# Second attention of a two-layer gated block on one core: score products moved from padded full-height operands to strips of 32 array rows

## The reference

```python
def _L1_xattn_ref(q, k, v, gamma):            # q = layernorm(x); k = v = ctx
    B, Dq, Lq = q.shape                       # 32, 64, 256
    h = 8; dq = Dq // h                       # 8 heads of 8 rows
    qh = q.reshape(B, h, dq, Lq); kh = k.reshape(B, h, dq, Lk); vh = v.reshape(B, h, dv, Lk)
    qk = jnp.einsum('bhdq,bhdl->bhql', qh, kh) * scale
    sm = jax.nn.softmax(qk, axis=-1)
    ret = jnp.einsum('bhql,bhdl->bhdq', sm, vh)
    return gamma * ret.reshape(B, Dv, Lq)
x = x + jnp.tanh(g_xattn[1]) * _L1_xattn_ref(_layernorm(x, axis=-1), ctx, ctx, gamma)
```

## Time and profile before

| | |
|---|---|
| median of 3 runs | 817.76 us (816.28 to 818.45) |
| span of the profiled execution, first to last instruction | 814.5 us |
| PE busy with matmuls, share of the span | 755.2 us, 93% |
| PE busy with weight loads | 576.9 us, 71% |
| DVE busy | 513.3 us, 63% |
| ACT busy | 435.3 us, 53% |
| POOL busy | 295.0 us, 36% |
| mean granted clock of TensorE | 0.975 of full speed |

### The profile page before, as it was taken

One profiled execution on the slowest core, in us unless ns is written; L12 is line 12 of the kernel. 1 busy time (PEld: TensorE's weight loads), 2 busy tenths in 40 slices (PEclk: granted clock), 3 DMA queues, 4 the chain that ended last, 5 costly groups with the idle time before them and its releaser, 6 DMA issues. The chain is left out here.

```text
span 814.5 us, 16953 instructions
## 1 busy us (share of the span) xinstructions
PE 755.2 (93%) x5377; PEld 576.9 (71%) x5377; DVE 513.3 (63%) x871; ACT 435.3 (53%) x862; POOL 295.0 (36%) x354
## 2 busy tenths in 40 slices
PE   4788889999995999999999999689999999999997
PEld 3677667888985666666666666367787778878776
DVE  3888857897797877887788787462344244253222
ACT  3888834344442777778777787633322332233221
POOL 3455542224446524433533443153222223213222
PEclk9999979999996899999999999889999999999999
DMA  5444410000004433433333331000000000000000
GB/s 146 119 112 128 116 59 1 1 0 0 1 21 127 131 99 97 113 109 94 110 106 100 94 112 44 1 1 1 1 1 27 1 1 26 0 0 0 27 1 27
DMA packets 48093, 43.88 MB, mean 54 GB/s; under 512 B 7860, under 2 KB 46356, under 8 KB 48052
## 3 DMA queue, kind: packets, MB, share of 16 engines
q1 hardware_dynamic: 45892, 37.46, 16.2%
q0 software_dynamic: 2160, 5.90, 2.6%
HBM read 27.99 MB, written 15.07 MB: 53 GB/s over the span
## 5 line engine op out<-in xcount | busy, mean ns | idle before, releaser
L1321 DVE TENSOR_REDUCE a_smax<-a_s 128x4 f32<-128x1024 f32 x128 | 154.4, 1209 | 46.6 <-PE a_s L1255 46.4
L1155 ACT ACTIVATE a_prob<-a_st 128x512 f32<-128x512 f32 x256 | 144.6, 591 | 34.9 <-PE a_st L1243 33.8
L1593 POOL TENSOR_TENSOR f_hs_lo<-f_hid,f_hs_hi 128x512 fp32r<-128x512 f32 (+1 forms) x56 | 73.3, 1308 | 197.4 <-ACT f_hs_hi L1539 197.4
L1243 PE MATMUL a_st<-qop,kop 128*128 128x256 f32 x512 | 120.7, 318 | 1.0 <-DMA qop<-a_neg_t 0.6
L1243 PEld LDWEIGHTS a_st<-qop,kop 128*128 128x128 f32 x512 | 77.2, 189 | 60.3 <-ACT a_prob L1155 44.2
L117 PE MATMUL f_bank<-wd_hi,f_hs_hi 128*128 128x256 f32 (+1 forms) x352 | 104.4, 297 | 7.2 <-POOL f_hs_lo L800 6.2
L1653 DVE TENSOR_TENSOR f_prod<-f_sg,f_bank 128x512 f32<-128x512 f32 x44 | 30.2, 687 | 128.1 <-PE f_bank L119 110.4
L1539 ACT ACTIVATE f_hs_hi<-f_hid 128x512 fp32r<-128x512 f32 (+1 forms) x56 | 35.4, 632 | 139.4 <-PE f_bank L119 99.8
L1255 PE MATMUL a_s<-kop,qop 127*128 127x256 f32 x512 | 104.9, 291 | 4.9 <-DVE a_smax L1321 2.6
L119 PE MATMUL f_bank<-wd_hi,f_hs_lo 128*128 128x256 f32 (+1 forms) x352 | 99.3, 282 | 0.0
L118 PE MATMUL f_bank<-wd_lo,f_hs_hi 128*128 128x256 f32 (+1 forms) x352 | 99.0, 281 | 0.0
(11 more groups left out here) (180 smaller groups left out, 1393.0 us busy)
## 6 DMA issues: line engine op xcount, KB each, us to landing
kop<-kop_rows SPq DMA_DIRECT2D x128, 48.0 KB
qop<-qop_rows SPq DMA_DIRECT2D x128, 48.0 KB
kop_rows<-k_hi SPq DMA_DIRECT2D x32, 128.0 KB, 2.3
qop_rows<-q_hi POOLq DMA_DIRECT2D x30, 128.0 KB, 2.6
x_all<-in_x SPq DMA_DIRECT2D x4, 512.0 KB, 4.7
ctx_t<-in_ctx SPq DMA_DIRECT2D x16, 128.0 KB, 2.0
kop_rows<-k_lo SPq DMA_DIRECT2D x16, 128.0 KB, 2.3
a_ctx<-in_ctx SPq DMA_DIRECT2D x16, 128.0 KB, 2.1
```

The source lines that it names most:

```text
L1155: act.activation(prob[:, u % 8], st_ps[u % 2][:], ACT.Exp, scale=SCALE1).then_inc(prob_ready, 1)
L1243: mm = pe.matmul(st_ps[u % 2][:, c * D:(c + 1) * D], lhsT=kop[t.slot][:, u // 4, c * P:(c + 1) * P], rhs=qop[t.slot][:, u // 4, u % 4], st ...
L1321: dve.tensor_reduce(smax[:, v.slot, 2 * j:2 * j + 2].rearrange("p u q -> p (u q)"), s_ps[j % 2][:].rearrange("p u (q n) -> p (u q) n", q=2 ...
L1593: pool.tensor_tensor(hs[1][0:r, c % 2], hid[0:r, c % 2], raw(hs[0][0:r, c % 2]), ALU.subtract).then_inc(hs_ready, 1)
```

## The change

The query operand loses its padding: `qop` is `[P, QUADS, D]`, with each unit's rows in the unit's own strip, as in `kop`. Its memset falls away. Both score products read only one strip: 24 rows for `s`, and 25 for `st`, as the row of maxima now lies in row 24 of each strip (partitions 24, 56, 88, 120). `tile_position` puts each product on the 32 array rows of its strip. The `s` products of a step are done in another order (`opposite`: unit u^2 in the place of u), and the four matmuls of a place alternate: st, s, st, s. The store of the maximum and the order within `neg` follow suit. All waits of a place now stand ahead of its four matmuls, and `st_done` is raised by the third of them.

```diff
-MROW = P - 1
+KROWS = QROWS + 1
...
-        self.q.append(sb(f"qop{n}", [P, QUADS, 4, D], F32R))
+        self.q.append(sb(f"qop{n}", [P, QUADS, D], F32R))
...
-        pool.memset(raw(self.k[slot][:]), 1.0)
-        pool.memset(raw(self.q[slot][:]), 0.0).then_inc(self.cleared, 1)
+        pool.memset(raw(self.k[slot][:]), 1.0).then_inc(self.cleared, 1)
...
-            dst = self.q[t.slot][v * UROWS:v * UROWS + QROWS, quads, v]
+            dst = self.q[t.slot][v * UROWS:v * UROWS + QROWS, quads]
...
+        def opposite(u):
+
+            return u ^ 2
...
-                sp.dma_start(raw(qop[t.slot][MROW:P, 2 * h:2 * h + 2]), neg_t[:, h]).then_inc(max_loaded[h][t.slot], 16)
+                sp.dma_start(raw(qop[t.slot][QROWS:P:UROWS, 2 * h:2 * h + 2]), neg_t[:, h]).then_inc(max_loaded[h][t.slot], 16)
...
-                        for c in range(DC):
-                            mm = pe.matmul(st_ps[u % 2][:, c * D:(c + 1) * D], lhsT=kop[t.slot][:, u // 4, c * P:(c + 1) * P],
-                                           rhs=qop[t.slot][:, u // 4, u % 4], start=True, stop=True)
-                        mm.then_inc(st_done, 1)
...
-                        for q in range(2):
-                            mm = pe.matmul(s_ps[j % 2][:, k, q * D:(q + 1) * D], lhsT=qop[v.slot][0:MROW, u // 4, u % 4, q * P:(q + 1) * P],
-                                           rhs=kop[v.slot][0:MROW, u // 4], start=True, stop=True)
-                        if k == 1:
-                            mm.then_inc(s_done, 1)
+                    for c in range(DC):
+                        if t.inside(TILES):
+                            strip = slice(u % 4 * UROWS, u % 4 * UROWS + KROWS)
+                            st = pe.matmul(st_ps[u % 2][:, c * D:(c + 1) * D], lhsT=kop[t.slot][strip, u // 4, c * P:(c + 1) * P],
+                                           rhs=qop[t.slot][strip, u // 4], start=True, stop=True, tile_position=(u % 4 * UROWS, 0))
+                        if v.inside(TILES):
+                            w = opposite(u)
+                            strip = slice(w % 4 * UROWS, w % 4 * UROWS + QROWS)
+                            sm = pe.matmul(s_ps[j % 2][:, k, c * D:(c + 1) * D], lhsT=qop[v.slot][strip, w // 4, c * P:(c + 1) * P],
+                                           rhs=kop[v.slot][strip, w // 4], start=True, stop=True, tile_position=(w % 4 * UROWS, 0))
+                    if t.inside(TILES):
+                        st.then_inc(st_done, 1)
+                    if v.inside(TILES) and k == 1:
+                        sm.then_inc(s_done, 1)
...
-                    src = smax[:, w_.slot, 8 * h:8 * h + 8].rearrange("p u q -> p q u")
+                    src = smax[:, w_.slot, 8 * h:8 * h + 8].rearrange("p (g v) q -> p q v g", g=2)
...
-                    dve.tensor_scalar(neg[:, h], src, -1.0, None, ALU.mult).then_inc(neg_ready, 1)
+                    dve.tensor_scalar(neg[:, h].rearrange("p q (v g) -> p q v g", g=2), src, -1.0, None, ALU.mult).then_inc(neg_ready, 1)
...
-                        dve.tensor_reduce(smax[:, v.slot, 2 * j:2 * j + 2].rearrange("p u q -> p (u q)"),
+                        dve.tensor_reduce(smax[:, v.slot, opposite(2 * j):opposite(2 * j) + 2].rearrange("p u q -> p (u q)"),
```

## The result

The changed kernel took 827.71, 827.83, 894.87 and 896.86 us, a median of 861.35 against 817.76 before. Over the two shorter executions alone the ratio is 1.0123 (interval 1.0103 to 1.0143), 1.2% slower; by the median of all four it is 5.3% slower. The two long ones have a mean granted clock of 0.79, the two short ones of 0.89, so the time goes with how long the clock stayed at half, and the spread is part of the result. The profiled execution is the first, with a span of 826.0 us. I had forecast 781.

The account below looks back on a forecast made before the run. PE was taken to set the pace at 15.84 us a step; minus 3.84 for sharing, plus 0.87 for borders and 0.4 for waits gives 13.3, saving 37 us over 14.8 steps: 781 us, range 767 to 819.

Parts of the forecast that it names:

- the step of 13.3 us: Changed stage at full clock: PE's 12.9 us plus 0.4 for waits, against 15.84 before, saving 37 us.
- Pairs stream together: Neighbouring score matmuls in different row strips share the array: 0.24 us saved per unit, 3.84 per step; chance 66%.
- The rival of serial loads: Weight loads of row strips run one after another, leaving only the new borders' cost: +13 us, 831; chance 15%.
- the other end: Bound of the score saving: a unit's four score products take the time of one, saving 5.8 us per step.
- Borders at the transposes: New changes of the array's form around the transposes behind units 2, 11 and 14: 0.87 us more per step.
- 12.9 for PE: PE's time per step after the change: 15.84 - 3.84 + 0.87, with DVE at 12.6 and ACT at 12.5.
- the allowance: Extra per step for waits: 0.1 for late maxima and 0.3 for DVE against `s`, 0.4 together.
- Maxima and operand loads: Rival: their waits, or the joined waits, hold the step at 14.5 to 15 us, 798 to 806; chance 10%.
- The joined waits: Waits ahead of `st` let a late maximum of pair j-2 also hold back `st` and ACT: 0.3 us a step allowed.
- my rival: The granted clock falls to half in the stage: steps of some 19.4 us, +52 us, 870; chance 4%.

Follow-up runs that it names:

- unshared strips: Changed kernel with unit u in the place of unit u, so a place's four score products lie in one strip: 969.18 us; on strips of 64 rows 1021.71 us.
- the burst: 30 whole-array products of 256 columns added in step 3: changed kernel 793.41 us, four units earlier 795.84 us; with unit u in the place of unit u 969.40 us.
- 64 rows and half the maximum: Strips of 64 rows, with the row maximum over only the first 128 of 256 scores: 779.12 us, ratio 0.9533 against the kernel before.
- the 64-row version: Changed kernel with strips of 64 rows for 32, query operands zero-padded for one neighbour: 781.67 us; with waits of `s` moved behind the first `st`, 783.23 us.
- memset alone: Changed kernel at 24 and 25 rows, with only the 32-row version's zeroing of the query operand added back: median 895.13 us.

## Why the prediction was wrong

The step that failed is the clock, which the sum put at no cost. The prediction read that it "is at full speed throughout the stage", took that over from before into the step of 13.3 us, and gave 4% to its fall. In the profiled execution the first 6.6 steps ran at half clock and took 20.64 us each, which is 49 us. The argument against it, that the value products "stay at full height, and PE stays without gaps", was shown wrong: with unshared strips, of 25 rows with and without the burst and of 64 rows, PE had no gap and the clock stayed at half or went back to it. It was not a fall either. The first line of the earlier trace rows has 0.58 for the stretch ahead of the stage: the clock enters at half, and the products of this stage have to bring it back.

- **Pairs stream together**: right. `st` and `s` start 0.01 apart, and their loads overlap. The rival of serial loads fell. The saving per pair of units, 1.72 - 1.19 = 0.53, is a little over the forecast's 0.48, as the next unit's products overlap too. In part that is the other end that the prediction had named, four in the time of one.
- **Borders at the transposes**: right in kind, 0.31 against 0.14 on leaving. The step of 13.3 came out as 13.25. That it did so is not proof of its terms: with 64 rows and half the maximum it was 13.1, where the forecast had 12.9 for PE, and undoing DVE's part gave 0.2, where the allowance was 0.4.
- **Maxima and operand loads** didn't bind. The joined waits did in the way described, for 9 us in 95, and undoing them in the 64-row version gave nothing. Order and joined waits on the padded operands cost 2.8 us (1.9 to 3.8), where I had nothing.
- **The clock**: my rival had the half clock, with pairs together, and a step of 19.4. It measured 20.64, as changes of form take longer at half clock: a unit with value products lasts 1.73 us (318.32 to 320.05 in the trace), of which 1.26 was for its products, so 0.47 where I had kept 0.34. The rival put the half clock over the whole stage, 870. The executions that seem never to have risen took 895 and 897; that the median of 861 lies near 870 is luck, as it is the middle of two pairs, 828 and 896.

What decides over the clock, as far as the runs show: both kernels enter the stage at half, behind a wait of PE of 2.2 us between the stages. It stands at half from 258.9 to 269.2 before, and from 261.4 on after. Before, full-height products had it back after these 10.3 us, unshared as they are and with PE busy for only 7.7 of them. Of the short products only shared ones brought it back: in the profiled executions at 280.3 (64 rows), 283.6 (32), 347 (28), and at 408, at 283 or not in the stage (25). Without sharing it did not come back in the stage, at 64 rows or 25. A burst gives it back, and shared products of 25 rows then held it, where unshared ones didn't. All runs fit this. Rows at the same sharing, and sharing at the same rows, were each changed alone. But an unshared step is also longer (25.60 and 28.88 us at half clock against 20.64), so the full-height value products fill less of it; whether sharing itself or that share counts was not tried apart. Why executions of one kernel differ with 25 and 28 rows is open too.

The Trainium skill ("TensorE: Matmul & The Clock Gate", Part 3) gives as the way out for short contractions to run several matmuls at the same time in one array, each in its own tile. The trace agrees, with 0.01 us between the starts of `st` and `s`. The runs add that what happens to the clock may take more than the gain.

## What to carry to other kernels

A product on fewer rows takes the same time (0.38 and 0.28 us with 24, 25, 63 and 64 rows) and may cost the clock. When packing the array, look at the granted clock first, and keep neighbours both sharing and as tall as they can be, with zeros if need be. Here the change with 24 and 25 rows was slower by 1.2% at its best and 5.3% by the median, and padding to all 32 rows of a strip, or to 64, made it 4.2 and 4.4% faster than before. Take a clock from the stage of before as a measurement of that stage's products, not as a constant, and where PE enters a stage from a wait, price the half clock over all of it.

## What the hardware showed that was not expected

- A loaded, gapless PE at half clock for 440 us: from 280 to 720 us with 64 rows unshared, busy for 440.00 of them.
- Seven rows of zeros and ones, 32 in place of 25 (31 in place of 24 for `s`), moved the median from 895 (memset alone) to 783 us.
- A full clock can be kept where it isn't regained: shared products of 25 rows held it for 190 us behind a burst, and without one had not brought it back in 137 us.
- Products of the next unit, in strips that are free, start before the second products of the unit ahead, out of the order in which the program issues them: four start within 0.01 us at 405.90 in the changed kernel.
